# Linear attention with an FP4 feed-forward on one core: where GpSimd's copy of q waits, and how the weights are prepared

## The reference

```python
q = relu(x @ Wq).reshape(b, s, 64, 64) * SCALE;  k = relu(x @ Wk).reshape(...);  v = (x @ Wv).reshape(...)
kv  = einsum('bsid,bsjd->bsdj', k, v)          # as written in the reference
out = einsum('bsid,bsdj->bsij', q, kv)
q_norm = einsum('bsid,bsd->bsi', q, k.sum(axis=2))
x = layernorm(x + (out / (q_norm[..., None] + 1e-6)).reshape(b, s, 4096) @ Wo + bo)
# feed-forward: fp4(a) = nearest of 0, .5, 1, 1.5, 2, 3, 4, 6 times max|block|/6, with a's sign
h = silu(fp4(x) @ fp4(w_gate).T) * (fp4(x) @ fp4(w_up).T)
x = layernorm(x + fp4(h) @ fp4(w_down).T)
```

## Time and profile before

| | us |
|---|---|
| median of 3 runs | 2490.99 (2480.89 to 2496.33) |
| the profiled execution | 2491.44 |
| its span | 2489.7 |
| outside its span | 1.7 |
| granted clock of PE, mean | 0.941 of full |

### The profile page before, as it was taken

One profiled execution on the slowest core, in us unless ns is written; L12 is line 12 of the kernel. 1 busy time (PEld: TensorE's weight loads), 2 busy tenths in 40 slices (PEclk: granted clock), 3 DMA queues, 4 the chain that ended last, 5 costly groups with the idle time before them and its releaser, 6 DMA issues.

```text
span 2489.7 us, 88190 instructions
## 1 busy us (share of the span) xinstructions
PE 2144.2 (86%) x37963; PEld 2015.4 (81%) x37963; DVE 2088.1 (84%) x3943; ACT 1483.3 (60%) x2634; POOL 1702.6 (68%) x2068
## 2 busy tenths in 40 slices
PE   1788988988988988888898898898898898898875
PEld 1787978888888888888888888888888798898874
DVE  8679888888888888888888888888888988888874
ACT  3556656656656656656666666665665665665651
POOL 6566766766776776776776676676676676676673
PEclk9899999999999999999999999999999999999986
DMA  4456556556556556556656656655645655655651
GB/s 147 103 122 143 112 121 138 121 117 145 121 116 142 120 115 141 123 113 140 129 113 134 130 114 133 133 117 126 147 105 124 135 114 126 146 110 121 147 109 41
DMA packets 523211, 308.28 MB, mean 124 GB/s; under 512 B 275590, under 2 KB 497734, under 8 KB 522310
## 3 DMA queue, kind: packets, MB, share of 16 engines
q1 hardware_dynamic: 522822, 302.65, 56.5%
HBM read 17.38 MB, written 4.19 MB: 9 GB/s over the span
## 4 chain that ended last, share of the span: by engine, by line
PE 47%; DVE 32%; issue 10%; POOL 5%; ACT 5%; DMA 1%; SPq 0%; DVEq 0%; POOLq 0%; ACTq 0%
PE ps L408 13%; PE ps L361 10%; PE ps L362 9%; PE ps L363 9%; DVE k_acc L722 9%; DVE v_st L740 9%; DVE k_acc L733 3%; PE ps L462 3%; POOL o_st L1061 3%; POOL q_nat L1051 3%; ACT v_st L539 2%; PE ps L463 2%; DVE q L757 2%; PE ps L447 1%; DVE o L781 1%
## 5 line engine op out<-in xcount | busy, mean ns | idle before, releaser
L1061 POOL TENSOR_TENSOR o_st<-o,o_st 128x256 bf16<-128x256 f32 x1024 | 662.3, 680 | 50.9 <-ACT o_st L622 50.1
L1051 POOL TENSOR_TENSOR q_nat<-q,q_nat 128x512 bf16<-128x512 f32 x512 | 590.5, 1175 | 89.2 <-ACT q_nat L598 89.2
L622 ACT CAST o_st<-o 128x256 bf16<-128x256 f32 x1024 | 352.6, 403 | 285.2 <-DVE o L781 281.9
L361 PE MATMUL ps<-v_st,q_bd 128*128 128x66 bf16 x4096 | 465.9, 201 | 51.8 <-DVE o L781 25.1
L361 PEld LDWEIGHTS ps<-v_st,q_bd 128*128 128x128 bf16 x4096 | 423.4, 115 | 77.6 <-DVE o L781 41.4
L362 PE MATMUL ps<-v_st,q_bd 128*128 128x66 bf16 x4096 | 461.5, 200 | 0.0
L363 PE MATMUL ps<-v_st,q_bd 128*128 128x66 bf16 x4096 | 460.2, 199 | 0.0
L362 PEld LDWEIGHTS ps<-v_st,q_bd 128*128 128x128 bf16 x4096 | 424.8, 117 | 1.5 <-issue 0.4
L363 PEld LDWEIGHTS ps<-v_st,q_bd 128*128 128x128 bf16 x4096 | 422.3, 116 | 0.0
L598 ACT CAST q_nat<-q 128x512 bf16<-128x512 f32 x512 | 292.0, 618 | 210.6 <-DVE q L757 210.4
L361 PE MATMUL ps<-xT,w_q 128*128 128x128 bf16 x2048 | 377.5, 226 | 45.9 <-DVE k_acc L722 40.0
(11 more groups left out here) (133 smaller groups left out, 5710.0 us busy)
## 6 DMA issues: line engine op xcount, KB each, us to landing
q_bd<-q_nat SPq DMA_DIRECT2D x256, 256.0 KB, 3.9
swap<-v_st SPq DMA_DIRECT2D x64, 576.0 KB, 6.5
v_st<-v_st SPq DMA_DIRECT2D x64, 576.0 KB, 5.2
v_st<-swap SPq DMA_DIRECT2D x64, 576.0 KB, 5.4
swap<-o_st SPq DMA_DIRECT2D x64, 512.0 KB, 4.4
o_st<-o_st SPq DMA_DIRECT2D x64, 512.0 KB, 8.3
o_st<-swap SPq DMA_DIRECT2D x64, 512.0 KB, 5.9
x_in<-in_L_attn_x SPq DMA_DIRECT2D x64, 64.0 KB, 5.4
```

The lines of the kernel that those rows point to most:

```text
L361: nc.tensor.matmul(dst, lhs(0), rhs(0), start=True, stop=False)
L622: last = nc.scalar.copy(ost[1 - t.par][:, 0, :, a, g * G:(g + 1) * G, :], src[:, a])
L1051: last = nc.gpsimd.tensor_tensor(qnat[:, 1, a, :, e, :], src[:, a], qnat[:, 0, a, :, e, :], ALU.subtract)
L1061: last = nc.gpsimd.tensor_tensor(lo[:, :, a], src[:, a], hi[:, :, a], ALU.subtract)
```

## The change

- POOL's `q_stay` waits, in turns with `back` work, for x1 as well (`s_x1`), that is for DVE's `x_one`.
- DVE's order: `stats_1` ahead of the low halves of v, `mean_1` behind `v_lo(0)`, `x_one` ahead of `v_lo(3)`, `k_add` 2 and 3 one step earlier among the steps of x's FP4. At the end of the turn `norm_o(6)` stands behind `q_scale(3)` and `h_round`, and `h_grid` ahead of `scale_o(7)`. ACT's `h_step` stands ahead of `o_hi(5)`, POOL's `h_back` ahead of `o_lo(7)`.
- The low halves of Wv and Wk are made by DVE in place of POOL, between the quantiser of gate and up and the first turn.
- The quantiser of the weights is that of the activations: divide by the block's scale, take the top bits, round by adding and subtracting a large number; 7 passes over the data in place of 14.
- w_down is loaded last, quantised at the end of turn 0 on DVE, transposed by PE in turn 1 into TB1 and copied by ACT in turn 1. Wo goes to another staging tile (`o_st[1]`), its high half is made by ACT in turn 0 behind `k_first`, its low half by POOL after its other early work. The first load is x.

```diff
         def _(sp):
+            sp.dma_start(x_in[:, :], x_t[0:T, :]).then_inc(s_x, 16)
             for g, w in enumerate((w_gate, w_up)):
...
-            sp.dma_start(dn_raw, w_down).then_inc(s_fload, 16)
-            sp.dma_start(x_in[:, :], x_t[0:T, :]).then_inc(s_x, 16)
...
+            sp.dma_start(dn_raw, w_down).then_inc(s_dload, 16)
@@ PE
                 if t.is_(0):
                     pe.wait_ge(s_ffnw, 1)
-                    transpose_down_weights()
...
                 project(t, "k", 3)
+                if t.is_(1):
+                    transpose_down_weights()
@@ ACT
                 k_first(t)
+                if t.is_(0):
+                    weight_o_hi()
...
                 k_sums(t)
+                if t.is_(1):
+                    down_weights()
...
                 o_hi(t, 4)
+                h_step(t)
                 o_hi(t, 5)
                 q_hi(t, 3)
                 o_hi(t, 6)
-                h_step(t)
                 o_hi(t, 7)
@@ DVE
+            def quantise(raw, q, np_):
+                nb, w = raw.shape[1] // BLK, raw.shape[1]
+                raw, q, sc, rs = raw[0:np_], q[0:np_], w_sc[0:np_, 0:nb], w_sc[0:np_, 64:64 + nb]
                 link(nc.vector.tensor_reduce(sc, blocks(raw), AX.X, ALU.max, apply_absolute_value=True))
                 link(nc.vector.tensor_scalar(sc, sc, 1.0 / 6.0, 1e-12, ALU.mult, ALU.max))
                 link(nc.vector.reciprocal(rs, sc))
+                link(nc.vector.scalar_tensor_tensor(out=blocks(raw), in0=blocks(raw), scalar=BELOW_ONE,
+                                                    in1=per_block(rs, raw), op0=ALU.mult, op1=ALU.mult))
+                link(nc.vector.tensor_tensor(q.bitcast(I32), raw.bitcast(I32),
+                                             consts[0:np_, 2:3].bitcast(I32).to_broadcast([np_, w]), ALU.bitwise_and))
+                link(nc.vector.scalar_tensor_tensor(out=q, in0=q, scalar=MAGIC_STEP,
+                                                    in1=consts[0:np_, 3:4].to_broadcast([np_, w]), op0=ALU.mult, op1=ALU.add))
+                link(nc.vector.tensor_tensor(raw, q, raw, ALU.add))
+                link(nc.vector.tensor_tensor(q, raw, q, ALU.subtract))
                 nc.vector.tensor_tensor(blocks(q), blocks(q), per_block(sc, raw), ALU.mult).then_inc(s_wquant, 1)
...
+            for k in "vkq":
+                dve.wait_ge(s_whi[k], 1)
+                for hh in range(2):
...
+                        last = nc.vector.tensor_tensor(lo, split_src[k][:, :, hh], hi, ALU.subtract)
+                last.then_inc(s_wlo[k], 1)
...
                 residual_1(t)
-                v_lo(t, 0)
-                v_lo(t, 1)
                 stats_1(t)
                 before_mean_1(t)
+                v_lo(t, 0)
+                mean_1(t)
+                v_lo(t, 1)
                 v_lo(t, 2)
-                mean_1(t)
+                x_one(t)
                 v_lo(t, 3)
-                x_one(t)
                 k_add(t, 1)
                 x_max(t)
+                k_add(t, 2)
                 x_lo(t)
                 x_scale(t)
-                k_add(t, 2)
+                k_add(t, 3)
                 x_recip(t)
-                k_add(t, 3)
                 x_norm(t)
...
-                norm_o(t, 6)
                 scale_o(t, 5)
                 q_scale(t, 3)
+                h_round(t)
+                norm_o(t, 6)
                 norm_o(t, 7)
                 recip(t, 6, 2)
                 scale_o(t, 6)
+                h_grid(t)
                 scale_o(t, 7)
-                h_round(t)
-                h_grid(t)
+                if t.is_(0):
+                    down_quantise()
@@ POOL
-            for k in "vk":
-                pool.wait_ge(s_whi[k], 1)
-                for hh in range(2):
-                    hi, lo = (wmat[k][:, l].rearrange("p e (h m) -> p e h m", h=2)[:, :, hh] for l in range(2))
-                    last = nc.gpsimd.tensor_tensor(lo, split_src[k][:, :, hh], hi, ALU.subtract)
-                last.then_inc(s_wlo[k], 1)
...
             nc.gpsimd.memset(vst[1][:, 1, :, :, HALF:VS], 0.0).then_inc(s_clear, 1)
+            pool.wait_ge(s_whi["o"], 1)
+            nc.gpsimd.tensor_tensor(w_o[:, 1, :], stage["o"], w_o[:, 0, :], ALU.subtract).then_inc(s_wlo["o"], 1)
             pool.wait_ge(s_store, 16)
...
                 if t.back:
                     pool.wait_ge(s_rs1, t.b + 1)
+                    pool.wait_ge(s_x1, t.b + 1)
...
                 o_lo(t, 6)
+                h_back(t)
                 o_lo(t, 7)
-                h_back(t)
                 q_lo(t, 3)
```

More of the change, by code:

```diff
@@ L522, in _, with weight_o_hi, down_weights @@
             weight_hi("q")
[L523 to L528, removed]
+            def weight_o_hi():
+                act.wait_ge(s_wload["o"], 32)
+                nc.scalar.copy(w_o[:, 0, :], stage["o"]).then_inc(s_whi["o"], 1)
+            def down_weights():
+                act.wait_ge(s_wT, 2)
+                for c, (k0, kn) in enumerate(DOWN):
+                    last = nc.scalar.copy(w_dn[0:kn, c, :], TB1[0:kn, c * DIM:(c + 1) * DIM])
+                last.then_inc(s_ffnw, 1)
             def v_hi(t, c):
@@ L590, in q_hi @@
                     return
-                if c == 0 and t.is_(0):
-                    act.wait_ge(s_wlo["o"], 1)
                 if c == 0 and t.attend:
@@ L616, in o_hi @@
                     return
+                if g == 0 and t.is_(2):
+                    act.wait_ge(s_wlo["o"], 1)
                 if g == 0 and t.back:
@@ L685, in _ @@
                 link(nc.vector.reciprocal(rs, sc))
-                link(nc.vector.scalar_tensor_tensor(out=ab, in0=raw, scalar=-1.0, in1=raw, op0=ALU.mult, op1=ALU.max))
-                link(nc.vector.tensor_tensor(blocks(ab), blocks(ab), per_block(rs, raw), ALU.mult))
-                link(nc.vector.tensor_scalar(q, ab, MIDS[6], 2.0, ALU.is_gt, ALU.mult))
-                for k in (5, 4):
-                    link(nc.vector.scalar_tensor_tensor(out=q, in0=ab, scalar=MIDS[k], in1=q, op0=ALU.is_gt, op1=ALU.add))
@@ L691, in _ @@
-                link(nc.vector.tensor_scalar(mask, ab, MIDS[0], None, ALU.is_gt))
-                for k in (1, 2, 3):
-                    link(nc.vector.scalar_tensor_tensor(out=mask, in0=ab, scalar=MIDS[k], in1=mask, op0=ALU.is_gt,
-                                                        op1=ALU.add))
-                link(nc.vector.scalar_tensor_tensor(out=q, in0=mask, scalar=0.5, in1=q, op0=ALU.mult, op1=ALU.add))
-                link(nc.vector.tensor_scalar(mask, raw, 0.0, 2.0, ALU.is_ge, ALU.mult))
@@ L706, in _ @@
-            for hh in range(2):
-                hi, lo = (wmat["q"][:, l].rearrange("p e (h m) -> p e h m", h=2)[:, :, hh] for l in range(2))
-                last = nc.vector.scalar_tensor_tensor(out=lo, in0=split_src["q"][:, :, hh], scalar=SCALE, in1=hi,
-                                                      op0=ALU.mult, op1=ALU.subtract)
-            last.then_inc(s_wlo["q"], 1)
-            dve.wait_ge(s_wlo["q"], 1)
+                link(nc.vector.scalar_tensor_tensor(out=blocks(raw), in0=blocks(raw), scalar=BELOW_ONE,
+                                                    in1=per_block(rs, raw), op0=ALU.mult, op1=ALU.mult))
@@ new lines, in quantise @@
+                nc.vector.tensor_tensor(blocks(q), blocks(q), per_block(sc, raw), ALU.mult).then_inc(s_wquant, 1)
+            dve.wait_ge(s_fload, 32)
+            quantise(gu_raw, gu_q, WP)
+            dve.wait_ge(s_xhi, 1)
+            nc.vector.tensor_tensor(xT[0][:, 1, :], TB1[:, 0:T], xT[0][:, 0, :], ALU.subtract).then_inc(s_xlo, 1)
+            for k in "vkq":
+                dve.wait_ge(s_whi[k], 1)
+                for hh in range(2):
+                    hi, lo = (wmat[k][:, l].rearrange("p e (h m) -> p e h m", h=2)[:, :, hh] for l in range(2))
+                    if k == "q":
+                        last = nc.vector.scalar_tensor_tensor(out=lo, in0=split_src["q"][:, :, hh], scalar=SCALE, in1=hi,
+                                                              op0=ALU.mult, op1=ALU.subtract)
+                    else:
+                        last = nc.vector.tensor_tensor(lo, split_src[k][:, :, hh], hi, ALU.subtract)
+                last.then_inc(s_wlo[k], 1)
```

33 lines of the change are left out of this document (11 added, 22 removed).

## The result

| | us |
|---|---|
| median after (4 runs) | 2367.22 (2365.52 to 2368.57) |
| median before (4 runs) | 2493.66 (2480.89 to 2498.93) |
| ratio | 0.950, 95% interval 0.946 to 0.954 |
| span of the profiled execution, before and after | 2489.7 and 2363.7 |
| turn 3 to turn 64 (61 turns), before and after | 2265.1 and 2147.7: 37.13 and 35.21 a turn |

The account below looks back on a forecast made before the run. PE was taken to wait for the last k fold, late because x_one stood behind POOL's copy of q. 2491.4 - 104 (stall) - 58 (clock) - 13 (start) = 2316, plus 2 for delays: 2318 us, range 2280 to 2384.

Parts of the forecast that it names:

- The stall and what is next: Turns 3 to 63: x_one no longer stands behind POOL's copy; k_sum starts 1.44 us behind out_group(0) in place of 3.15.
- The term of 104 us: Gain in the 61 turns from the shorter wait ahead of k_sum: 1.7 us each, bounds 0 to 134.
- both were released by the same event, rs1: In the turn, x_one and POOL's copy of q start on one event, so x_one stands behind the copy.
- a wait there is hidden: x_scale in the turn: held by a late copy, it costs nothing, as DVE must wait for out_group(0) anyway.
- 75 in all, come with stretches at the lower level (1.2 GHz) or with other waits: Mean turns exceed the full-clock turn by 1.23 us; of the 75, 58 were taken as gained, bounds 0 to 75.
- After `k_sum` every step is shifted together: Rest of the turn behind k_sum: all steps move sooner alike, since q_scale, the casts and slots hang on ks.
- The start: Ahead of turn 3: v_lo(0) 28.4 us sooner, 7.0 lost in folds, 8.4 in down's quantiser; gain 13 (5 to 26).
- the 2 us set aside for delays: Added to the forecast sum for small delays in turns, taking 2316 to 2318 us.
- The clock keeps its stretches: Rival on the turns: lower-clock stretches remain, so their gain is missing; 2374 us, chance 0.17.
- x_one late by its own order: Rival: x_one ahead of v_lo(3) waits for POOL and delays k2, about 1 us a turn; 2379 us, chance 0.1.
- The slower rival: POOL's copy shuts out v_lo(3) or k_add(1) too, k2 comes 3.5 us later; 2588 us, chance 0.03.

Follow-up runs that it names:

- head_order: Kernel before with only VectorE's new order at the head of the turn, stats_1 to x_norm, without the wait for x1: 2399.36 us, ratio 0.962.
- no_wait: Kernel after without the one line that makes GpSimd's copy of q wait for x1: 2352.74 us, ratio 0.945.
- only_wait: Kernel before with one line added, GpSimd's copy of q also waits for x1: 2432.74 us, ratio 0.976.
- y_split: y_psum with half of ScalarE's last q_stay (64 x 1024 values) given to GpSimd behind its own copy: 2337.62 us, ratio 0.938.
- y_psum: Kernel after with the second residual r2 kept in PSUM, so y has one input in SBUF: 2299.01 us, ratio 0.922.
- start_only: Kernel after with all three iteration orders of the kernel before and without the copy's wait, new weight preparation kept: 2485.68 us, ratio 0.996.
- best: y_split with k_add(3) ahead of x_scale, w_down quantised between low halves of Wv and Wk, Wo's low half in turn 1: 2244.99 us, ratio 0.902.
- y_late: Kernel after with y moved two steps later, behind h_round instead of behind scale_o(4): 2407.24 us, ratio 0.966.

## Why the prediction was right, and where it was off

- **The stall and what is next.** Right. `x_one` left the path, the group waits for ACT, DVE for the group (0.98 in turn 12), 1.46 us from group to `k_sum` where 1.44 was forecast, full-clock turns of 34.15 where 34.2 was. The term of 104 us (61 x 1.7) stands: 61 x (35.90 - 34.15) = 107.
- **What released the two.** The step "both were released by the same event, rs1" failed. POOL was; DVE came from `v_lo(3)`. So I gave the gain to the wait, while `head_order` and `no_wait` show that the order alone brings it, `only_wait` that the wait alone brings it less half a us. Either suffices, so the sum did not suffer. That is luck: of the order the prediction asked only what it might cost.
- **x_scale.** I held that a wait there is hidden. In the order of the change it fell beside nothing (0.16 us in turns 3 to 63), as forecast. Where it did fall into the copy (`only_wait`, `y_split`) it was not hidden.
- **The clock: the step that failed.** The prediction says that "75 in all, come with stretches at the lower level (1.2 GHz) or with other waits", and took 58 of them as gained. The measured term is 11: before, the 61 turns took 75 us more than 61 full-clock turns, and after the change still 64. Of the 75 some 63 were the clock, but six turns were `y`, 2.0 us each, and its 4.2 us stood in the trace as the maximum of L890; I had no row of it. Of the 64 after, 16 are the clock (18 x 0.9) and 48 are `y` (20 x 2.4). So the clock gave back 47 and `y` took 36 more. The 17 us that the forecast left over were matched by the clock's 16, but by luck: 17 of the 18 turns with a stretch follow a long `y`, and with `y` short one turn is left (`y_psum`). "After `k_sum` every step is shifted together" left out `y` and its race for the port. That is nearly the whole distance from the point: this term fell 47 short and the start 4, while the turns gave 3 more and the 2 us set aside for delays were not needed. Whether the new order made `y` lose more often is not shown, since the same order gave 6 and 12 (`start_only`).
- **The start.** 13 forecast, 9 in the trace, 10 in `start_only`. `v_lo(0)` came at 31.44 and not at 28.9, as Wq's high half was not ready; the folds lost 7.1 as taken (8.59 - 1.48, the latter from `best`), and down's quantiser took 9.4 (65.18 to 74.62 in the trace) where 8.4 were priced. Turn 3 begins up to 5 us apart in executions with the same preparation, so the match of the sum is no closer than that.
- **The rivals.** "The clock keeps its stretches" gave 2374, 7 us from the 2367 measured, and would have looked right by its time; but the clock gave back 47 us, and the trace shows another cause. "x_one late by its own order" did not occur (held in none of 61). The slower rival, that the copy shuts out `v_lo(3)` or `k_add(1)`, fell: both keep their 1.2 us (at most 1.23 in all of them). Its price was near, by another way: `x_one` held ahead of `v_lo(3)` costs 3.4 a turn (`head_order`).

## What to carry to other kernels

Look at the minimum and the maximum of every VectorE operation that reads two SBUF tiles, or is a tensor_scalar on SBUF, wherever GpSimd works beside it: a maximum ten times the minimum, as in L820 and L890 here, is a stall that the profile counts as busy time. A wait or an order can win such a race. For an operation with two inputs the safe way here was to leave it, by keeping one of them in PSUM; for the tensor_scalar `x_scale` it was another place in the order. When a stall is removed, the other races on the engine can turn out otherwise, so count them before and price them in. And look at what stands behind a turn with a stall: here the next turn paid for it too, at the lower clock.

## What was not expected of the hardware

- A small operation that loses does not get the port at the next hand-over but waits for a gap in GpSimd's work: `y` started within one POOL instruction and was held through four more (turn 13), yet in the next turn, starting at the same distance into the same instruction (0.11 and 0.13 us), it got it at the hand-over and took 0.70. What decides was not found: `y` lost 6 of 60 times before, 12 in `start_only`, 15 in `no_wait`, 20 in the kernel after and in `only_wait`, 28 in `head_order`, 44 in `y_late`. In the preparation VectorE and GpSimd took turns all the same: three passes beside GpSimd's `q_lo` and copy took 1.36, 1.36 and 3.81 us.
- A stall of VectorE came with a lower clock of TensorE a turn later: with `y` short the clock stayed at its higher level in 60 of 61 turns (`y_psum`), in 43 before that change, and 17 of the 18 others directly followed a turn with a long `y`.
